# Issuing a small index load on ScalarE's DMA queue instead of at the head of SyncE's

## What is computed

```python
def _L0_cond_ref(x, condition, weights):        # x (64, 32, 512), condition (64,), weights (16, 32, 32)
    W = weights[condition]
    return jnp.einsum('bct,bcd->bdt', x, W)
...
def _L0_ffn_ref(x, W_base, b_base, W_gate, A, B):
    result = jnp.einsum('bnd,od->bno', x, W_base) + b_base
    logits = jnp.einsum('bnd,ed->bne', x, W_gate)
    probs = jax.nn.softmax(logits.astype(jnp.float32), axis=-1)
    top_p, top_i = jax.lax.top_k(probs, TOP_K)
    top_p = top_p / jnp.sum(top_p, axis=-1, keepdims=True)
    ...
    h = jnp.einsum('bnd,erd->bner', x, A)
    hw = h * route_w[..., None]
    delta = jnp.einsum('bner,eor->bno', hw, B)
    return result + delta * SCALING
x = x + _L0_ffn_ref(_L0_cond_ref(x, itok_B_0_15, L0_cond_weights), ...)
```

## Time and profile before

| | before |
|---|---|
| median of three runs | 95.51 us |
| the profiled execution: device time | 95.24 us |
| the profiled execution: span from first to last instruction | 93.4 us |
| PE busy | 89.8 us (96%), 643 instructions |
| PE weight loads busy | 86.2 us (92%) |
| DVE busy | 65.2 us (70%) |
| ACT busy | 23.5 us (25%) |
| POOL busy | 16.6 us (18%) |
| queue q1 (loads and stores of SP) | 5760 packets, 10.25 MB |
| queue q10 (loads of ACT) | 144 packets, 0.07 MB |
| queue q0 (gathers of POOL) | 448 packets, 0.23 MB |

### The profile page before, as it was taken

The page is one execution under the profiler, slowest core; times in us unless marked ns, Lnnn a source line. Parts: engine busy times, 40 slices in busy tenths (PEclk is TensorE's granted clock), DMA queues, the critical chain, the costliest instruction groups (busy, mean ns, idle before and its releaser), DMA issues.

```text
span 93.4 us, 1811 instructions
## 1 busy us (share of the span) xinstructions
PE 89.8 (96%) x643; PEld 86.2 (92%) x643; DVE 65.2 (70%) x228; ACT 23.5 (25%) x55; POOL 16.6 (18%) x29
## 2 busy tenths in 40 slices
PE   6999999999999999999999999999999999999980
PEld 2387999999999999999999999999999999999970
DVE  2895988768675758768675767767675969867660
ACT  5067630313113050313213040312213040311210
POOL 5158512301204040300304040210300000000000
PEclk9999999999999999999999999999999999999999
DMA  2999173513307060422407060332506020302023
GB/s 37 287 338 381 45 216 118 185 50 118 113 20 211 0 218 20 127 104 103 129 5 227 7 217 15 118 117 84 146 11 224 0 112 0 112 7 112 0 112 112
DMA packets 6360, 10.65 MB, mean 114 GB/s; under 512 B 1008, under 2 KB 1616, under 8 KB 6352
## 3 DMA queue, kind: packets, MB, share of 16 engines
q1 hardware_dynamic: 5760, 10.25, 33.2%
q0 software_dynamic: 448, 0.23, 1.1%
q10 hardware_dynamic: 144, 0.07, 0.2%
HBM read 6.35 MB, written 4.19 MB: 113 GB/s over the span
## 4 chain that ended last, share of the span: by engine, by line
PE 88%; DMA 5%; SPq 2%; DVE 1%; ACT 1%; issue 0%
PE main_ps L520 53%; PE y_ps L507 13%; PE main_ps L536 11%; DMA w_raw<-w_all 5%; PE main_ps L596 5%; PE main_ps L602 3%; PE hwT_ps L530 2%; SPq L208 1%; DVE x_sb L488 1%; ACT w_hi L282 1%; SPq L211 0%; PE main_ps L635 0%; SPq L213 0%
## 5 line engine op out<-in xcount | busy, mean ns | idle before, releaser
L520 PE MATMUL main_ps<-w_hi,y_hi 128*128 128x320 f32 x112 | 27.0, 322 | 0.1
L520 PE MATMUL main_ps<-w_lo,y_hi 128*128 128x320 f32 x112 | 26.8, 321 | 0.0
L520 PE MATMUL main_ps<-w_hi,y_lo 128*128 128x320 f32 x112 | 25.8, 311 | 0.0
L259 POOL DMA_INDIRECT mixw<-cond_w,row_ids x14 | 13.8, 985 | 47.6 <-PE y_ps L507 45.3
L520 PEld LDWEIGHTS main_ps<-w_hi,y_lo 128*128 128x128 f32 x112 | 19.0, 188 | 0.0
L520 PEld LDWEIGHTS main_ps<-w_lo,y_hi 128*128 128x128 f32 x112 | 18.5, 189 | 0.1
L520 PEld LDWEIGHTS main_ps<-w_hi,y_hi 128*128 128x128 f32 x112 | 18.0, 190 | 0.6 <-ACT w_hi L282 0.6
L507 PE MATMUL y_ps<-mix,x_sb 128*128 128x128 f32 x124 | 16.6, 276 | 0.1
L507 PEld LDWEIGHTS y_ps<-mix,x_sb 128*128 128x128 f32 x124 | 15.6, 191 | 0.2 <-DVE mix L365 0.2
L292 ACT ACTIVATE second<-top 128x1 f32<-128x1 f32 x16 | 4.7, 295 | 42.7 <-DVE top L388 42.7
L415 DVE TENSOR_TENSOR hwT_lo<-hwT_ps,hwT_hi 128x128 fp32r<-128x128 f32 x16 | 4.7, 292 | 12.9 <-ACT hwT_hi L299 12.9
(11 more groups left out here) (66 smaller groups left out, 87.2 us busy)
## 6 DMA issues: line engine op xcount, KB each, us to landing
x_sb<-x SPq DMA_DIRECT2D x16, 256.0 KB, 2.9
out<-x_sb SPq DMA_DIRECT2D x15, 256.0 KB, 2.1
w_raw<-w_all SPq DMA_DIRECT2D x4, 324.0 KB, 4.9
b_raw<-b_lora SPq DMA_DIRECT2D x1, 256.0 KB, 5.6
bias_sb<-bias SPq DMA_DIRECT2D x1, 256.0 KB, 4.0
out<-x_sb SPq DMA_DIRECT2D x2, 128.0 KB, 1.8
mixw<-cond_w,row_ids POOLq DMA_INDIRECT x14, 2.6
table<-cond_w ACTq DMA_DIRECT2D x1, 64.0 KB, 2.0
```

Of the source, the lines that this page charges most:

```text
L259: pool.indirect_dma_start(mixw[:, t, :], None, cond_w, bass.IndirectOffsetOnAxis(row_ids[:, t:t + 1], 0))\
L520: last = pe.matmul(main_ps[t % 2][:, half, 0:n_cols], y, w[:, half * HALF:half * HALF + n_cols], start=i == 0, stop=i == STEPS - 1)
```

## The change

The load of `cond_sb` leaves the head of SP's queue and becomes ACT's first instruction, ahead of the load of `table`. SP's first DMA is then x tile 0, and every later one of SP follows one place earlier. Nothing else is edited.

```diff
--- before.py
+++ after.py
@@ -210,7 +210,6 @@
             def load_w(c):
                 sp.dma_start(w_raw[:, c, :], w_chunks[c, :, :]).then_inc(w_landed[c], 16)
 
-            sp.dma_start(cond_sb[:, :], cond).then_inc(cond_landed, 16)
             load_x(0)
             load_w(0)
             load_x(1)
@@ -299,6 +298,7 @@
                 act.activation(hwT_hi[t % 2][:, :], hwT_ps[t % 2][:, 0:P], ACT.Copy)\
                     .then_inc(hwT_hi_ready, 1)
 
+            act.dma_start(cond_sb[:, :], cond).then_inc(cond_landed, 16)
             act.dma_start(table[:, 0, :, :], cond_w.rearrange("(p k) d -> p k d", k=K)).then_inc(table_landed, 16)
             split_w(0)
             for (y, hi, _), done, ready in zip(first_halves(), (first_y_done, y_done),
```

## The result

The changed kernel takes 98.00 us (median of six runs, 97.37 to 98.67) where the kernel before takes 95.53 (six runs). The ratio is 1.027, with a 95% interval of 1.0235 to 1.0301. The forecast was slower, 96.2 us; the direction was right and the size, +0.7 us, was a third of the measured +2.5. The time lies outside the range of 95.3 to 97.0. Three single executions in the whole record lie far above all others (112.98 us of the kernel before, 179.55 of e4, 311.34 of e3), and nothing is read from them.

A forecast was written before the change was run, and what follows sets the result against it. PE's dense work was taken to bound the kernel: a table 1.3 us late, less 0.57 us of slack, moves the end by +0.73, so 95.51 + 0.73 = 96.24, rounded 96.2 us. The range was 95.3 to 97.0.

The forecast's parts named there:

- What bounds the kernel: PE, busy 89.8 of 93.4 us; a change at the start counts only by when PE's dense work begins.
- The slack of 0.57 us: PE's two waits for `w_hi`, 0.33 and 0.24 us, by which the conditions and table chain could slip.
- The load chain: SP's loads of x and w, split by ACT: weights land 0.22 us earlier, 0.44 at the very most.
- The table's issue: On ACT the conditions' load goes first, so the table is issued 0.44 us later, with no slack in the trace.
- The table's way through the DMA engines: Small loads alternate packet by packet with SP's big loads; table late by 1.3 us, issue included, 1.8 at most.
- the forecast's own formula: Table delay on the DMA engines: 0.44 us issue plus turns of both small loads, 2 x 0.8 - 0.2, up to 1.8 us.
- the lower value: Table delay with only its own nine turns counted, 0.44 + 0.8 = 1.2 us; 1.3 was taken, near it.
- the second rival: DMA engines take whole shares in turn: end moves by 0 to +0.37 us, to 95.5 to 95.9; chance 0.23.
- the likeliest case: Table 1.3 us late, main steps on PE at 8.23, end moved by +0.73 us, 96.2 us; chance 0.45.
- TensorE's clock rises later: PE idles before the picks, mixing takes up to twice as long: up to +1.85 us, middle 97.0; chance 0.10.
- The table isn't held by x: On the DMA engines small packets slip through; table only 0.44 us later, end -0.13 us, 95.4; chance 0.17.
- The table runs only when q1 is empty: ACT's queue served only when SP's is empty; table lands near 10 us, kernel over 102 us; chance 0.03.

The follow-up runs named there:

- e4: Kernel before without the two matmuls on constants behind own_cond, no load touched; 96.25 us, ratio 1.0089.
- e3: Changed kernel with the table loaded at the head of SP's queue ahead of x tile 0, conditions still first on ACT; 95.28 us, ratio 0.9977.
- e7: Kernel before with x tile 0 issued by ACT behind the table, SP's later loads one place earlier; 95.57 us, ratio 1.0010.
- e6: Changed kernel with ACT's two loads the other way round, table and then conditions; 97.81 us, ratio 1.0288.
- e9: Changed kernel with the table loaded as two halves, the same bytes in more packets; 99.25 us, ratio 1.0364.
- e2: Changed kernel with an extra, unused 8 KB load of the conditions at the head of SP's queue, before x tile 0; 96.74 us, ratio 1.0116.
- e10: Changed kernel with w 0 ahead of x tile 0 on SP's queue; 98.09 us, ratio 1.0315.
- e1: Changed kernel with PE's idle stretches filled by more matmuls on constants, before and behind own_cond; 96.73 us, ratio 1.0135.
- e5: Kernel before with three instead of five matmuls on constants ahead of own_cond and none behind, no load touched; 96.14 us, ratio 1.010.

## Why the prediction was right or wrong

**What bounds the kernel: right.** PE's dense work is the end of all chains, and the end moved by what its start moved, less the slack. The slack of 0.57 us was right: both waits are gone after, and 3.28 us at the first main step became 2.66 at the step (2, 0).

**The load chain: right in what it gains, too small in size.** The weights were taken as 0.22 us earlier, 0.44 at the most. ACT's split of w 0 starts at 4.66 instead of 4.93, 0.27 us. But w 1, issued at 2.12, landed 4.2 us later, at 6.3, where it had landed at 7.34: 1.0 us earlier. The engines moved 392 and 374 GB/s in the microseconds from 3 and from 4, where they had moved 332 and 323; why, no run shows. That this would gain nothing beside a late table was right: w 1 and w 2 lay ready while ACT waited for PE's mixing, and its split of w 1 began at 9.42. What the earlier weights would be worth by themselves stays open, as e7 doesn't isolate them.

**The table's issue: right as a time, but not a term of its own.** 0.44 us later, as the issue rows say, and each 0.1 us of the table was nearly 0.1 us of the mixing (2.14 became 1.95). But the 0.44 us doesn't add to the rest: the table was queued by 1.63, long before the engines began with q10 at 2.45.

**The table's way through the DMA engines: the right mechanism, a size too small. This is the first step that failed.** Turns packet by packet were the forecast, and the counts of 82 to 81 show them; e6 and e9 show that packets and not bytes count. But I took 1.3 us with 1.8 as the upper end, and 2.14 was measured. Two things were missed. In the changed kernel, 32 packets of x tile 0 come first, and until 2.45 us nothing of the other queue starts, where it had started at 1.7; the row that I used, 320 to 336 GB/s, is of the later, full stretch, and there was no term for the start. And I took the value near the lower end, because the conditions "start at the same instant as x tile 0 and some of them get through before it": none did. By the trace after, q10 starts 0.75 us later than before, and its 18 turns at 0.1 us end at 4.3, where its nine had ended below 2.4: 1.9 of the 2.14 us. With the turns of both loads the forecast's own formula gave 1.8, so 0.5 of the missing 0.84 is the choice of the lower value and 0.3 is what had no term. The rule of the Trainium skill, DMA: Bandwidth & Descriptors, section "Queues, rings and completion order", that an engine drains a packet of several descriptors before it turns, was the second rival, with 95.5 to 95.9 us. Read with the profile's packets as its descriptors, the trace speaks against it here: q10's packets of 64 bytes and q1's of 2 KB alternate, 81 to 82 in half a microsecond.

**The clock: named, priced in the wrong place. This is the second step that failed: the likeliest case has it at nothing.** The rival "TensorE's clock rises later" had a chance of 0.10 as a case of its own, with up to 1.85 us on top. It was there, with 1.33 us. The fault is one of reasoning: it was listed beside the late table, when the late table brings it about. Given a table 1.3 us late, PE's idle time follows from the same rows. In all five kernels with a table (or, in e6, the conditions) late by 1.75 us or more and no added filling (the changed one, e2, e6, e9, e10), the profiled execution has 0.93 us for the first four weight loads. e1 has 0.52 with the table as late and PE filled, and e5 has 0.93 with the table on time and PE idle for 0.55 us before own_cond and 0.68 before the picks. No run has the table 1.3 us late, so how often the clock would have been in time there isn't shown, and e3's profiled execution shows that it can be late with no idle time too. With both terms as measured the sum is 1.95 + 1.33 - 0.57 = 2.7, where the forecast had 1.3 + 0 - 0.57 = 0.73.

**The other rivals.** "The table isn't held by x" fell, since L338 started at 4.85, not before 3.3. "The table runs only when q1 is empty" fell too: q10 is served while q1 is full.

**The range.** It left the clock's case mostly out, and its top came from a sum without the start of the queue.

## What to carry to other kernels

A small load that a long chain hangs on must be on its way before any big load is issued on any queue: another engine's queue isn't a way past it, and there each of its packets pays for one big packet. These runs show that for small loads of up to 64 KB behind or beside 256 and 324 KB. Giving a queue a place earlier is worth only the wait that it removes at the end, here 0.57 us at most, and it must be set against everything that is thereby no longer first. And when a chain gets longer, ask what the engine at its end does in the meantime: here PE's idle time cost as much again as the wait itself, and filling it with useless matmuls won 1.3 us back.

## What the runs showed of the hardware

- SP's and ACT's queues, with big packets waiting in SP's, get the DMA engines packet for packet, and not byte for byte: 82 packets of up to 2 KB against 81 of at most 64 bytes in half a microsecond, and 64 of up to 2.6 KB against 65 of mostly 512 bytes in another. 128 packets more in ACT's queue, with 16 for the semaphore, cost 0.66 us (e9).
- The first 32 packets of a big load, two for each engine on average, took 0.6 to 0.7 us of each engine (94.3% of 0.75 us in the changed kernel, 123% of 0.5 us in e2), and nothing of ACT's queue started meanwhile. That is over 0.3 us a packet, where packets of the same load later took 0.08 (82 packets, 86.0% of 0.5 us). The stretch isn't always that long: in e9 and e10 the first packets of ACT's queue start between 2.0 and 2.2 us, yet own_cond starts at 3.79 and 3.97, against 3.86 in the changed kernel. That it is the wait for the first reads is an inference.
- TensorE's pace has to be read from the instructions. The windows of the changed kernel over the slow mixing, 8 to 10.2 us, say:

```profile
8.00:9.00 1.00, 1.00 (x6) 1.00 0.69 262
9.00:10.20 1.20, 1.20 (x8) 1.00 0.10 14
```

The fourth number, the granted clock, is 1.00, while weight loads in the same stretch take nearly twice what they take in the kernel before. I had used that column as a sign of a full clock; at the start of this kernel it isn't one.
